# Inverse lengths of queries and keys: one GpSimd power over 16 columns a tile in place of two over 8

## The chip, the cores and the metric

The kernel runs on one core of a Trainium2 chip. The metric is the device time of one execution in microseconds. Several runs of a kernel are compared by their median.

## The reference

Sixteen sequences of 256 tokens with 128 features pass through six layers: a local-attention feed-forward (its output halved and added), a full attention with relative positions, the first again, a mixture of 64 experts, a state-space layer, and the experts again. The change lies in the first of them. There each token's projection is split into 8 heads of 64, queries and keys are divided by their length, and then rotated:

```python
def l2norm(t):
    return t / jnp.clip(jnp.linalg.norm(t, axis=-1, keepdims=True), 1e-12)
q = l2norm(q) * qs
k = l2norm(k) * ksc
q, k = rotary_xpos(q, k)
o = local_attention(q, k, v)
```

The layer has a depth of 2, and it is run twice.

## The kernel before

Two sequences (512 tokens, four tiles of 128) form a group; there are eight. Stages follow each other: `first_and_third` (local attention beside the experts of another group), `second` (full attention beside the state-space layer), `first_and_third` again. The groups are staggered, so most stages run two streams side by side. The order of the work is written out by hand for each engine.

`LocalFfn.run` (L1738) orders a stage. It has four passes (two layers of depth, two sequences each), each with two tiles of 128 tokens. A pass is projected (`project_*`), attended (`attend_*`) and mixed (`mix_*`), and the three phases of different passes overlap in rounds of eight steps r. Between them `beside` issues steps of the experts. A stage of the kind "first" in the middle of the run is entered with a `carry`: its pass 0 was projected in the stage before. All other stages are entered without one. Their pass 0 is projected at the entry, all steps in a row: VectorE runs `project_vector` for its four steps and then `beside.vector(dve, 2)` (L1861 to L1863); GpSimd runs `project_gpsimd` for both tiles (L1832); TensorE runs its five steps with filler matmuls between them (`keep_busy`, L137; L1750 to L1756). In the rounds, VectorE's steps come at r = 1 to 4 and GpSimd's tiles at r = 1 and 3.

The steps of one tile are these. TensorE projects queries, keys and values (L1380). ScalarE copies them (L1406, L1401) and squares queries and keys (L1409). VectorE sums the squares of each head to 16 lengths (L1433), clips them (L1435), and rotates: for the queries L1419, L1420, L1421, with the second step the same three lines for the keys, then adds the keys' two parts (L1441) and multiplies the keys by their inverse lengths (L1445). All these VectorE operations from L1419 on read two tensors of SBUF. GpSimd raises the clipped sums of squares to the power -0.5 in two instructions of 8 columns, keys first (L1452), adds the queries' parts (L1454) and multiplies the queries by their inverse lengths (L1458). TensorE transposes keys, then queries (L1387), in each of its steps 3 and 4, and ScalarE copies the result (L1412).

The semaphore `inv_norm` rises with each power. VectorE's key product waits for the first of a tile's two, GpSimd's query product for the second:

```python
dve.wait_ge(self.inv_norm, 2 * tile + 1)      # L1443
pool.wait_ge(self.inv_norm, 2 * tile + 2)     # L1456
```

After the tiles, attention reads the transposed keys and queries: scores (L1480) on a mask (L1476), their maxima on VectorE (L1577), exponentials on ScalarE (L1555), transposes and products on TensorE (L1509, L1520). Routing of the experts is a chain on VectorE (L625 to L644) with one exponential on ScalarE (L579); then each pair of experts has matmuls (L562, L568), a tanh (L586), a gate on VectorE (L654) and a product with the routing weights on GpSimd (L594). The state-space stages use GpSimd for sums of 1024 columns (L829, L844).

Of the kernel before, what the change touches and what calls it, by code (L numbers as in the profile page):

```python
# [10 lines left out]
ALU = mybir.AluOpType  # L11
# [12 lines left out]
DEPTH, LH, LD, WINDOW = 2, 8, 64, 64  # L24
# [1292 lines left out]
class LocalFfn:  # L1317
# [105 lines left out]
    def project_vector(self, dve, i, step):  # L1423
        v = self.nc.vector
        l, t = i // GROUP_SEQS, step // 2
        i -= self.first
        tile, lens = 2 * i + t, self.lens[t]
        if step % 2 == 0:
            dve.wait_ge(self.squared, tile + 1)
            if i >= 1:  # L1430
                dve.wait_ge(self.q_rotated, tile - 1)
                dve.wait_ge(self.projected, 10 * (i - 1) + 8 + 2 * t)
            v.tensor_reduce(lens, self.sine[t].rearrange("p (h d) -> p h d", d=LD), AX, ALU.add).then_inc(self.summed, 1)  # L1433
            dve.wait_ge(self.summed, tile + 1)
            v.tensor_scalar(lens, lens, 1e-24, None, ALU.max).then_inc(self.clipped, 1)  # L1435
            self.rotary(l, t, 0).then_inc(self.split, 1)
        else:
            self.rotary(l, t, 1).then_inc(self.k_split, 1)
            dve.wait_ge(self.k_split, tile + 1)
            keys = self.cosine[t][:, INNER:2 * INNER]  # L1440
            v.tensor_tensor(keys, keys, self.sine[t][:, INNER:2 * INNER], ALU.add).then_inc(self.k_added, 1)  # L1441
            dve.wait_ge(self.k_added, tile + 1)
            dve.wait_ge(self.inv_norm, 2 * tile + 1)  # L1443
            keys = keys.rearrange("p (h d) -> p h d", d=LD)
            v.tensor_tensor(keys, keys, lens[:, LH:].unsqueeze(2).broadcast_to([128, LH, LD]), ALU.mult).then_inc(self.k_rotated, 1)  # L1445

    def project_gpsimd(self, pool, i, t):
        b, tile = self.b, 2 * (i - self.first) + t
        lens, queries, sine = self.lens[t], self.cosine[t][:, 0:INNER], self.sine[t]
        pool.wait_ge(self.clipped, tile + 1)  # L1450
        for half in (lens[:, LH:], lens[:, 0:LH]):
            pool.tensor_tensor(half, half, b.minus_half[:].broadcast_to([128, LH]), ALU.pow).then_inc(self.inv_norm, 1)  # L1452
        pool.wait_ge(self.split, tile + 1)
        pool.tensor_tensor(queries, queries, sine[:, 0:INNER], ALU.add).then_inc(self.added, 1)  # L1454
        pool.wait_ge(self.added, tile + 1)
        pool.wait_ge(self.inv_norm, 2 * tile + 2)  # L1456
        queries = queries.rearrange("p (h d) -> p h d", d=LD)
        pool.tensor_tensor(queries, queries, lens[:, 0:LH].unsqueeze(2).broadcast_to([128, LH, LD]), ALU.mult).then_inc(self.q_rotated, 1)  # L1458

# [545 lines left out]
```

## Time and profile before

| | |
|---|---|
| median of three runs | 4873.61 us (4861.64 to 4876.70) |
| profiled execution | 4871.84 us, its span 4869.5 us |
| mean granted TensorE clock | 0.928 |
| tiles (one for each pass, two tiles each, 16 stages) | 128, with 256 powers |

The profile comes from one execution. A page has the busy time of each engine over the span, the costliest groups of instructions, and for each the idle time of the engine just before them, with the operation that ended it. PE is TensorE, DVE is VectorE, ACT is ScalarE, POOL is GpSimd. In a timeline, the first number is the start in us from the span's start, the second the duration; `x2` is two instructions in a row shown as one; a bracket gives the idle time before and what released the engine. An instruction's start is when the engine takes it up after its waits; one that is held back by another engine while running shows a longer duration.

### The profile page before, as it was taken

How to read it: one execution, taken by the hardware profiler on the slowest of the kernel's cores; microseconds unless marked ns; L12 is line 12 of the kernel's file. 1: busy time of each engine (PE TensorE's matmuls, PEld its weight loads, DVE VectorE, ACT ScalarE, POOL GpSimd, SP SyncE). 2: the span in 40 equal slices, each digit the busy share in tenths (PEclk: the TensorE clock that was granted, in tenths of full speed). 3: DMA queues.
4: the chain of work that ended last, by engine and by line, in shares of the span. 5: the costliest groups of instructions: out<-in, count | busy, mean ns of one | idle time of the engine just before them, and what ended most of it. 6: DMA issues, size and time to landing. Idle time of an engine off the chain costs nothing. (4 is left out here: it accounts for less than half of the span.)

```text
span 4869.5 us, 54706 instructions
## 1 busy us (share of the span) xinstructions
PE 4023.7 (83%) x17172; PEld 2422.5 (50%) x17172; DVE 3013.0 (62%) x5743; ACT 2787.0 (57%) x6184; POOL 2063.3 (42%) x1342
## 2 busy tenths in 40 slices
PE   6788898788878888888987988878887888889846
PEld 4446554455445554455544555445544555445412
DVE  4326666666576674766657666666747667476464
ACT  4465657555576555665665655755557555666332
POOL 2103244444264451644436434444436444165334
PEclk9898999999999999999999999999999999999867
DMA  3020013111131111210121111301113111221212
GB/s 102 1 89 1 22 50 122 30 44 40 34 122 41 35 46 63 86 49 29 58 85 61 53 30 49 122 29 44 38 36 122 41 35 49 68 76 49 81 47 75
DMA packets 188824, 274.01 MB, mean 56 GB/s; under 512 B 23448, under 2 KB 102900, under 8 KB 188532
## 3 DMA queue, kind: packets, MB, share of 16 engines
q1 hardware_dynamic: 186340, 268.72, 17.2%
q8 instruction: 147, 2.41, 0.2%
q10 hardware_dynamic: 2192, 1.70, 0.1%
q14 instruction: 145, 1.19, 0.1%
HBM read 215.54 MB, written 54.79 MB: 56 GB/s over the span
## 5 line engine op out<-in xcount | busy, mean ns | idle before, releaser
L594 POOL TENSOR_TENSOR work<-work 128x512 f32<-128x512 f32 x512 | 668.5, 1307 | 1200.8 <-DVE work L654 1117.5
L1452 POOL TENSOR_TENSOR work<-work,minus_half 128x8 f32<-128x8 f32 x256 | 469.5, 1848 | 545.2 <-DVE work L1435 542.9
L654 DVE SCALAR_TENSOR_TENSOR work<-work,psum 128x512 f32<-128x512 f32 x528 | 362.1, 686 | 412.9 <-ACT work L586 411.8
L562 PE MATMUL psum<-work,w_up 128*128 128x512 f32 x1024 | 546.2, 616 | 79.5 <-DVE work L654 76.0
L1555 ACT ACTIVATE work<-psum,work 128x128 f32<-128x128 f32 (+1 forms) x1024 | 392.3, 397 | 367.8 <-DVE work L1577 367.4
L586 ACT ACTIVATE work<-psum 128x512 f32<-128x512 f32 x528 | 315.3, 598 | 453.7 <-PE psum L562 433.4
L568 PE MATMUL psum<-work,w_down 128*128 128x512 f32 x1024 | 536.3, 606 | 5.5 <-POOL work L594 5.5
L1520 PEld LDWEIGHTS psum<-work 128*128 128x128 f32 x3072 | 388.6, 197 | 55.9 <-issue 54.1
L1520 PE MATMUL psum<-work 128*128 128x64 f32 x3072 | 410.3, 278 | 0.9 <-DVE work L1587 0.3
L1380 PE MATMUL psum<-wqkv,xn 128*128 128x512 f32 x768 | 374.8, 613 | 30.2 <-DVE xn L1685 26.3
L906 DVE TENSOR_TENSOR_SCAN work<-work,psum 128x256 f32<-128x256 f32 x512 | 323.1, 673 | 72.8 <-issue 35.1
L1509 PE MATMUL psum<-ident,work 128*128 128x128 f32 x1536 | 246.6, 285 | 140.0 <-ACT work L1555 110.6
L1509 PEld LDWEIGHTS psum<-ident,work 128*128 128x128 f32 x1536 | 185.1, 145 | 325.5 <-ACT work L1555 218.2
L844 POOL TENSOR_TENSOR pair<-pair,work 128x1024 f32<-128x1024 f32 x128 | 301.5, 2355 | 94.2 <-DVE work L829 85.4
L568 PEld LDWEIGHTS psum<-work,w_down 128*128 128x128 f32 x1024 | 195.7, 193 | 256.2 <-issue 218.3
L1641 PE MATMUL psum<-sq,w 128*128 128x256 f32 (+1 forms) x768 | 219.9, 429 | 73.1 <-DVE sq L1706 54.4
L1577 DVE TENSOR_REDUCE work<-psum 128x2 f32<-128x384 f32 (+1 forms) x384 | 212.4, 594 | 96.7 <-PE psum L1480 96.7
L562 PEld LDWEIGHTS psum<-work,w_up 128*128 128x128 f32 x1024 | 182.7, 194 | 173.0 <-DVE work L654 103.3
L829 POOL TENSOR_TENSOR work<-work,rows 128x1024 f32<-128x1024 f32 x28 | 66.1, 2361 | 417.4 <-DVE work L906 417.4
L1012 PE MATMUL psum<-rel_k,work 128*128 128x384 f32 x512 | 199.3, 517 | 45.5 <-ACT work L1099 27.2
L1433 DVE TENSOR_REDUCE work<-work 128x16 f32<-128x1024 f32 x128 | 155.4, 1214 | 126.4 <-ACT work L1409 125.5
L1406 ACT COPY work<-psum 128x512 f32<-128x512 f32 x256 | 148.6, 597 | 145.3 <-PE psum L1380 145.3
(228 smaller groups left out, 8503.7 us busy)
## 6 DMA issues: line engine op xcount, KB each, us to landing
work<-expert_weight_rows SPq DMA_DIRECT2D x1024, 128.0 KB, 2.9
position_scores<-work SPq DMA_DIRECT2D x64, 768.0 KB, 3.5
work<-position_scores SPq DMA_DIRECT2D x64, 512.0 KB, 3.8
work<-state_readout_rows SPq DMA_DIRECT2D x72, 256.0 KB, 4.3
rows<-state_readout_rows SPq DMA_DIRECT2D x32, 256.0 KB, 3.9
sq<-state_readout_rows SPq DMA_DIRECT2D x24, 256.0 KB, 4.2
rows<-in_L_attn_q SPq DMA_DIRECT2D x8, 256.0 KB, 2.9
expert_weight_rows<-work SPq DMA_DIRECT2D x16, 128.0 KB, 2.3
```

Source lines behind the costliest of these rows:

```text
L562: nc.tensor.matmul(UP, b.w_up[:, p * 128:(p + 1) * 128], self.xn, start=True, stop=True).then_inc(self.up, 1)
L568: nc.tensor.matmul(SUM, b.w_down[:, q], self.gate_h[q % 3], start=q == 0, stop=False).then_inc(self.down, 1)
L586: nc.scalar.activation(self.tanh_h[p % self.turns][0:rows], bank(b, self.ups[p % self.turns])[0:rows], ACT.Tanh, scale=0.5).then_inc(self. ...
L594: pool.tensor_tensor(h, h, self.weights[p % self.SLOTS], ALU.mult).then_inc(self.gated, 1)
L654: v.scalar_tensor_tensor(out=self.gate_h[p % 3][0:rows], in0=self.tanh_h[p % self.turns][0:rows], scalar=1.0, in1=bank(b, self.ups[p % sel ...
L844: pool.tensor_tensor(self.sums, self.sums, self.state_pairs[n % 2], ALU.add).then_inc(self.added, 1)
L906: ins = v.tensor_tensor_scan(self.states[i % 4][:, at], self.decays[i % 2][:, at], drive[:, at], 0.0, ALU.mult, ALU.add)
L1380: nc.tensor.matmul(out, b.xn[:, at:at + 128], b.wqkv[:, l, part * INNER:(part + 1) * INNER], start=True, stop=True).then_inc(self.projecte ...
L1452: pool.tensor_tensor(half, half, b.minus_half[:].broadcast_to([128, LH]), ALU.pow).then_inc(self.inv_norm, 1)
L1509: ins = nc.tensor.transpose(bank(b, 2)[:, n * 128:(n + 1) * 128], flat[:, n * 128:(n + 1) * 128], b.ident[:])
L1520: ins = nc.tensor.matmul(bank(b, 3)[:, head * LD:(head + 1) * LD], self.probs_t[m % 2][:, n * 128:(n + 1) * 128], self.v_sb[i % 2][:, c, h ...
L1555: ins = self.nc.scalar.activation(out[:, x, -n:] if t else out[:, x], self.scores(m)[:, x], ACT.Exp, bias=self.neg_max[i % 2][:, slot:slot ...
```

## The change

The two powers of 8 columns become one of 16, over the whole tile `lens` (queries' lengths in columns 0 to 7, keys' in 8 to 15). Both waits on `inv_norm` become waits for this one instruction; the number of increments per tile falls from two to one. Nothing else is touched.

```diff
@@ project_vector
-            dve.wait_ge(self.inv_norm, 2 * tile + 1)
+            dve.wait_ge(self.inv_norm, tile + 1)
@@ project_gpsimd
-        for half in (lens[:, LH:], lens[:, 0:LH]):
-            pool.tensor_tensor(half, half, b.minus_half[:].broadcast_to([128, LH]), ALU.pow).then_inc(self.inv_norm, 1)
+        pool.tensor_tensor(lens, lens, b.minus_half[:].broadcast_to([128, 2 * LH]), ALU.pow).then_inc(self.inv_norm, 1)
@@
-        pool.wait_ge(self.inv_norm, 2 * tile + 2)
+        pool.wait_ge(self.inv_norm, tile + 1)
```

## Rows read from the trace of the kernel before

**Rows 1.** The page, part 1: busy time (share of the span), instructions of each engine

```profile
PE 4023.7 (83%) x17172; PEld 2422.5 (50%) x17172; DVE 3013.0 (62%) x5743; ACT 2787.0 (57%) x6184; POOL 2063.3 (42%) x1342
```

**Rows 2.** The page, part 5: the costliest groups; busy us, mean ns | idle before

```profile
L594 POOL TENSOR_TENSOR work<-work 128x512 f32<-128x512 f32 x512 | 668.5, 1307 | 1200.8 <-DVE work L654 1117.5
L1452 POOL TENSOR_TENSOR work<-work,minus_half 128x8 f32<-128x8 f32 x256 | 469.5, 1848 | 545.2 <-DVE work L1435 542.9
...
L844 POOL TENSOR_TENSOR pair<-pair,work 128x1024 f32<-128x1024 f32 x128 | 301.5, 2355 | 94.2 <-DVE work L829 85.4
```

**Rows 3.** The waits of TensorE: us in total, times, longest

```profile
PE psum L1387 <- POOL work L1458: 18.2, 17, 1.6
```

**Rows 4.** Timeline of VectorE, 894 to 916 us and near 4374: start us, us, what

```profile
896.02 0.17 DVE L1435 TENSOR_SCALAR work<-work 128x16 f32<-128x16 f32 x1
...
899.51 0.69 DVE L1445 TENSOR_TENSOR work<-work 128x512 f32<-128x512 f32 x1
...
901.45 1.55 DVE L1419 TENSOR_TENSOR work<-work,rope_w 128x512 f32<-128x512 f32 x1
902.93 0.42 DVE L1420 TENSOR_TENSOR work<-work,rope_w 128x256 f32<-128x256 f32 x1
...
905.72 0.69 DVE L1445 TENSOR_TENSOR work<-work 128x512 f32<-128x512 f32 x1
906.32 0.42 DVE L625 TENSOR_TENSOR work<-psum,expert_bias 128x256 f32<-128x256 f32 x1
...
908.32 0.61 DVE L633 TENSOR_TENSOR work<-work 128x256 f32<-128x256 f32 x1
...
912.76 1.28 DVE L1577 TENSOR_REDUCE work<-psum 128x4 f32<-128x512 f32 x2
...
4374.28 0.42 DVE L625 TENSOR_TENSOR work<-psum,expert_bias 128x256 f32<-128x256 f32 x1
```

**Rows 5.** Timeline of GpSimd, 896.2 to 909 us

```profile
896.28 3.62 POOL L1452 TENSOR_TENSOR work<-work,minus_half 128x8 f32<-128x8 f32 x2 [5.55 <-DVE work L1435]
899.87 1.47 POOL L1454 TENSOR_TENSOR work<-work 128x512 f32<-128x512 f32 x1
901.41 1.04 POOL L1458 TENSOR_TENSOR work<-work 128x512 f32<-128x512 f32 x1
902.41 3.70 POOL L1452 TENSOR_TENSOR work<-work,minus_half 128x8 f32<-128x8 f32 x2
906.08 1.45 POOL L1454 TENSOR_TENSOR work<-work 128x512 f32<-128x512 f32 x1
```

**Rows 6.** Timelines of ScalarE and TensorE, 910 to 914 us

```profile
913.54 0.37 ACT L1555 ACTIVATE work<-psum,work 128x128 f32<-128x128 f32 x1 [3.49 <-DVE work L1577]
...
910.64 1.16 PE L1480 MATMUL psum<-work 64*128 64x128 f32 x16
```

**Rows 7.** The instructions of three lines: ns min/median/max, first and last start us

```profile
L1452 POOL TENSOR_TENSOR work<-work,minus_half x256: 1628/2017/2129, 43.1 to 4495.8; 128x8 f32<-128x8 f32 x128
...
L1454 POOL TENSOR_TENSOR work<-work x128: 1256/1472/2131, 46.7 to 4497.4; 128x512 f32<-128x512 f32 x128
...
L1419 DVE TENSOR_TENSOR work<-work,rope_w x256: 674/684/1553, 42.9 to 4496.4; 128x512 f32<-128x512 f32 x128
```

**Rows 8.** TensorE by microseconds: length, busy (instructions), granted clock, DMA; and its timeline there

```profile
1099.00:1100.00 1.00, 0.00 (x0) 0.80 0.00 0
...
1100.79 2.50 PE L1641 MATMUL psum<-sq,w 128*128 128x256 f32 x5 [3.31 <-DVE sq L1706]
```

**Rows 9.** Timelines of GpSimd and VectorE, 1098 to 1106 us

```profile
1098.77 4.06 POOL L1452 TENSOR_TENSOR work<-work,minus_half 128x8 f32<-128x8 f32 x2 [2.69 <-DVE work L1435]
1102.80 1.79 POOL L1454 TENSOR_TENSOR work<-work 128x512 f32<-128x512 f32 x1
...
1102.77 0.69 DVE L1445 TENSOR_TENSOR work<-work 128x512 f32<-128x512 f32 x1
...
1105.12 0.48 DVE L1711 SCALAR_TENSOR_TENSOR work<-psum,vec_cols,work 128x256 f32<-128x256 f32 x1 [1.22 <-ACT work L1675]
```

## The prediction

> **What bounds the kernel now.** I read the totals first. TensorE works 83% of the span and GpSimd 42% [rows 1], so no engine is full: the end is set by chains of waits that run through all of them. The edited powers are GpSimd's second largest group, 256 instructions and 469.5 us [rows 2]. If every saved microsecond reached the end the change would be large, so the question is who waits for GpSimd's rotation. The table of TensorE's waits answers it: 17 waits, 18.2 us in all [rows 3]. All but these few of the 128 tiles are ready before TensorE asks. 18.2 us is 0.37% of the time, the ceiling of what earlier queries can give directly.
>
> The 17 waits lie in nine places: the entries of stages without a carry, where both tiles of pass 0 are projected with nothing between them. They start at 43.1 us [rows 7], at 359 and, in the groups after, from 896 to 4364. Seven of the nine have expert routing right behind the second tile on VectorE, the first at 906.32 and the last at 4374.28 [rows 4]; the other two, the one at 43.1 among them, have none. I take the entry at 896 as the pattern. GpSimd: power pair 896.28 to 899.90, addition L1454, multiplication L1458, then tile 1 the same way [rows 5]. VectorE runs without idle time from the clip at 896.02 to the score maxima at 912.76, and ScalarE's exponentials then wait 3.49 us for these maxima [rows 4, 6]. So behind the entry **VectorE's chain sets the pace**, not GpSimd's.
>
> The rows also show how the two engines disturb each other. L1419 on VectorE (two SBUF inputs) starts at 901.45, 0.04 after GpSimd's L1458, and takes 1.55 us where its median is 0.68; L1458 ends at 902.45, and L1419 ends 0.55 later [rows 4, 5, 7]. In the other order, L1445 starts at 899.51, 0.36 before L1454, and keeps its 0.69; L1454 then takes 1.47 instead of 1.26 [rows 4, 5, 7]. Whoever starts first keeps the other out to the end. During the power itself the rotations of VectorE are not stretched. The Trainium skill (SBUF — State Buffer, "Who interferes with whom") says the same as a rule: an exclusive lock between GpSimd and a VectorE instruction with two SBUF inputs, and issue order decides who blocks. By that rule, as by the rows, the order in which L1445 and L1454 start matters more here than the power's length.
>
> **The change, part by part.**
>
> *The power.* Two instructions of 8 columns take 2.02 and 1.63 us and together 3.62 [rows 5, 7]. The merged one costs the first plus eight more columns. No row shows 16 columns. From above: if nothing of the second instruction is fixed cost, 3.6 us. From below: if all of it is fixed, 2.0. The nearest fixed part is that of GpSimd's ordinary tensor_tensor: 1.307 us for 512 columns and 2.355 for 1024 leave 0.26 [rows 2], so the other 1.37 of the 1.63 is columns. I take 2.02 + 1.37 = **3.4 us**, 0.2 less than the pair, as these are the same engine and kind of instruction.
> The Trainium skill (GPSIMD Engine Reference, "Elementwise — side-by-side cycle accounting") gives about 2.6 cycles an element at 1.2 GHz, by which eight columns would cost 17 ns and the merged power 2.0 us; the sum by that is the second rival below.
>
> *The keys' wait.* Before, VectorE's key product L1445 needed only the first half, ready at 898.3; it started at 899.51 with no wait. Now it needs the whole power: 896.28 + 3.4 = 899.68, plus 0.08 for the signal (the lag from the clip's end at 896.19 to the power) = 899.76. That is only 0.25 later. But GpSimd's L1454 stands directly behind the power and needs no signal from VectorE; it follows its predecessor's end by minus 0.03 [rows 5]. It starts at 899.65, **ahead of** L1445, where it used to start 0.36 behind. It runs 1.27 us, to 900.92, and L1445 ends at 901.47 instead of 900.20: 1.27 late.
>
> *Tile 1.* Behind L1445 on VectorE stand the second reduction, the clip and the rotation. L1419 moves from 901.45 to 902.72. GpSimd's L1458 is over by then (about 902.4), so L1419 loses its stretch of 0.87 and the next operation, L1420, comes at 903.32 against 902.93: 0.39 late. The power of tile 1 now waits for the clip: 902.89 to 906.29. L1445 could start at 906.11, is released at 906.37 and finds L1454 (906.26 to 907.53) ahead again: it ends at 908.08 against 906.41, 1.67 late. Queued behind it are the routing (L625 on) and the maxima. L633 (0.61) has shown a stretch of 0.19 that goes, as L1458 is over. Net 1.48 us per entry, on the chain that ScalarE and through it TensorE wait for: 7 x 1.48 = **+10.4 us**.
>
> *The two other entries.* Nothing follows the product on VectorE. GpSimd's L1458 of tile 1 ends about 0.34 late (held by the locked L1445), and TensorE waits for that: +0.4 together.
>
> *TensorE's clock.* In an entry TensorE will now stand idle some 3 us between its filler and the key transposes, 1.5 more than before. A gap of 3.31 us comes with a fall of the granted clock (0.80 in one microsecond of it, on its way from 2.4 to 1.2 GHz) [rows 8]. The score matmuls (1.16 us for 16) [rows 6] would take up to twice as long, but VectorE's maxima are late anyway. Bounds: 0, and 7 x 1.2 = 8 us; I take 2, nearer to the covered case.
>
> *The other 110 tiles.* There L1445 starts 4.0 us or more after the power's start (shortest: 1102.77 behind 1098.77) [rows 9], so no new wait. The adds start 0.2 earlier, and operations locked behind them are free 0.2 earlier; most adds are themselves held by an L1419 that started first, so they don't move. Bounds -3 and 0, I take -1. In the tiles like the one at 1098 us L1445 (1102.77) starts only 0.03 before L1454; there the order flips too and costs VectorE about 0.9, but it idles 1.22 us before its next dependent step [rows 9], which covers it. Without that cover nine such tiles would cost 8 us.
>
> *Removed instruction and semaphore steps* cost and give nothing beyond the above; no DMA or queue of SyncE is touched.
>
> **Sum.** 10.4 + 0.4 + 2 - 1 = +11.8 us. The profiled execution took 4871.84 us (span 4869.5 and 2.3 around it), 1.8 below the median of the runs. 4871.8 + 11.8 + 1.8 = **4885.4 us**, 0.24% slower than 4873.61. A measurement of this kernel tells about 0.3%, 14.6 us, from no change, so this is the upper part of "no change".
>
> **The rivals.**
> 1. *The saving arrives* (faster). If L1445 keeps its turn, or its lateness reaches nobody, only GpSimd's shorter chain counts. With the power at 3.4 it gives 16 x 0.2 = 3 us, 4870, which is no change. To be faster the power must be near 2.0 us: then the 17 waits vanish, 18.2 us, and the time is **4855**. It decides at a saving of about 0.9 us a tile. Against it: L1454 starts ahead of L1445 for every length below 3.6.
> 2. *Columns nearly free and more collisions* (clearly slower). With a power of 2.0 both adds start inside VectorE's key steps, L1441 and L1445: two stretches of 0.87 a tile, 3.5 an entry, less 0.87 for L1419 and 0.2 for L633: 2.4 x 7 = 17 us, with the clock's 2 **4892**. For it: the same lock rows; against: it needs the low bound of the power.
> 3. *Late but covered.* The lock is as told but ScalarE or TensorE absorb the 1.5 us within the pass, or the power takes as long as before and the order stays mixed: **4873**. For it: 83% busy TensorE; against: TensorE idles behind exactly these exponentials.
> 4. *The change doesn't do what it says*: the merged instruction falls into a costlier form, over 4 us. Each 0.5 us above 3.6 costs two tiles in nine entries, 9 us. Little speaks for it.
>
> **How the numbers follow.** Forecast 0.62, rival 1 at its fast end 0.05, rival 2 0.13, rival 3 0.18, rival 4 0.02. The forecast's own spread is 4876 to 4895 (clock term, share absorbed), about two fifths of it beyond 4888.2. Slower: 0.62 x 0.4 + 0.13 x 0.8 + 0.02 = 0.37; faster 0.05; the rest, 0.58, within 0.3%. The range 4867 to 4899 leaves out the fast end and the worst of rival 2.
>
> **What would show it.** In the profile after: 128 powers of 128x16 at 3.4 us (2.0: rival 2 or 1; over 4: rival 4). At the nine entries L1445 of both tiles at 1.4 to 1.7 us instead of 0.69, starting about 0.1 after L1454; L1419 of tile 1 back at 0.68; the routing 1.5 to 1.7 us later behind the clip; the maxima still without idle time before them. TensorE's waits for L1458 stay near 18 us. The forecast is wrong if L1445 keeps 0.69, or if the pass behind the entry ends no later than before.

## The result and the profile after

| | kernel before | changed kernel |
|---|---|---|
| median, us (6 runs each) | 4876.23 (4861.64 to 4880.01) | 4915.15 (4906.55 to 4916.76) |
| ratio after / before | | 1.008, 95% interval [1.0066, 1.0094] |
| profiled execution, us | 4871.84 (span 4869.5) | 4915.54 (span 4913.0) |
| TensorE busy, us | 4023.7 | 4054.9 |

The change costs 39 us. The forecast was 4885.4 with a range up to 4899, so the sign was right, the "no change" that was put first (0.58) was not, and the time lies outside the range.

Part 1 of the page after, and the groups of its part 5 that answer to [rows 1, 2]; from the power on, line numbers are one lower than before:

```profile
PE 4054.9 (83%) x17172; PEld 2446.0 (50%) x17172; DVE 3061.3 (62%) x5743; ACT 2788.9 (57%) x6184; POOL 2012.7 (41%) x1214
...
L594 POOL TENSOR_TENSOR work<-work 128x512 f32<-128x512 f32 x512 | 667.0, 1303 | 1245.4 <-DVE work L654 1181.4
L1451 POOL TENSOR_TENSOR work<-work,minus_half 128x16 f32<-128x16 f32 x128 | 419.6, 3278 | 574.0 <-DVE work L1435 571.7
```

The joined power takes 3.28 us, and GpSimd is busy for 50.6 us less. All of that and more turns up elsewhere: VectorE is busy for 48 us more with the same 5743 instructions, and TensorE for 31 us more with the same 17172 matmuls. Nothing was added for either. So VectorE's instructions were stretched, and TensorE's ran longer: of the 43.5 us of span, 31.2 are matmuls that took more time and 12.3 are idle.

The waits of TensorE's transposes (total us, times, longest) show where its waits for the rotation went. Two rows of the kernel before, beside the one of [rows 3], and the three after:

```profile
PE psum L1387 <- ACT work L1412: 10.1, 7, 1.4
PE psum L1387 <- DVE work L1445: 6.5, 9, 1.4
```

```profile
PE psum L1387 <- ACT work L1412: 21.4, 7, 3.1
PE psum L1387 <- DVE work L1445: 17.9, 11, 2.5
PE psum L1387 <- POOL work L1457: 2.7, 10, 0.3
```

The waits for GpSimd's query product, 18.2 us before [rows 3], shrank to 2.7, but the three together grew from 34.8 to 42.0 us: the transposes now wait for the keys instead. At the entry shown below, the first tile's queries are ready some 0.2 us earlier behind the first clip and the second tile's no earlier at all, so little was there to gain.

**An entry.** The timelines of VectorE, GpSimd and TensorE at the entry that was the pattern of [rows 4, 5]:

```profile
900.54 0.17 DVE L1435 TENSOR_SCALAR work<-work 128x16 f32<-128x16 f32 x1
...
904.18 1.67 DVE L1445 TENSOR_TENSOR work<-work 128x512 f32<-128x512 f32 x1 [0.19 <-POOL work L1451]
...
910.65 1.67 DVE L1445 TENSOR_TENSOR work<-work 128x512 f32<-128x512 f32 x1 [0.19 <-POOL work L1451]
912.24 0.41 DVE L625 TENSOR_TENSOR work<-psum,expert_bias 128x256 f32<-128x256 f32 x1
...
919.33 1.29 DVE L1576 TENSOR_REDUCE work<-psum 128x4 f32<-128x512 f32 x2 [0.76 <-PE psum L1479]
```

```profile
900.79 3.28 POOL L1451 TENSOR_TENSOR work<-work,minus_half 128x16 f32<-128x16 f32 x1 [5.55 <-DVE work L1435]
904.04 1.26 POOL L1453 TENSOR_TENSOR work<-work 128x512 f32<-128x512 f32 x1
```

```profile
913.61 1.97 PE L1387 MATMUL psum<-ident,work 128*128 128x128 f32 x8 [3.06 <-ACT work L1412]
916.25 1.03 PE L1475 MATMUL psum<-mask_bf,ident_bf 128*128 128x512 bf16 x2 [0.68 <-ACT work L1412]
917.22 2.08 PE L1479 MATMUL psum<-work 64*128 64x128 f32 x16
```

GpSimd's addition starts at 904.04, VectorE's key product 0.14 later, and the product ends at 905.85, 0.55 after the addition. From the clip of tile 0 to the routing (L625) it is 11.70 us, against 10.30 before. TensorE then runs its 16 score matmuls in 2.08 us instead of 1.16 [rows 6], and the maxima (L1576) wait 0.76 for them. Before, they waited at none of the seven entries with routing; now they wait at two.

**A stage's end.** The same two engines and TensorE in the second of two tiles projected ahead, 10 us before the next stage:

```profile
1692.91 1.77 DVE L1441 TENSOR_TENSOR work<-work 128x512 f32<-128x512 f32 x1
1694.71 1.41 DVE L1445 TENSOR_TENSOR work<-work 128x512 f32<-128x512 f32 x1
1696.05 0.86 DVE L1710 SCALAR_TENSOR_TENSOR work<-psum,vec_cols,work 128x256 f32<-128x256 f32 x2
```

```profile
1689.62 3.28 POOL L1451 TENSOR_TENSOR work<-work,minus_half 128x16 f32<-128x16 f32 x1 [3.15 <-DVE work L1435]
1692.87 1.26 POOL L1453 TENSOR_TENSOR work<-work 128x512 f32<-128x512 f32 x1
```

```profile
1704.71 1.06 PE L1475 MATMUL psum<-mask_bf,ident_bf 128*128 128x512 bf16 x2
```

The addition is 0.04 us ahead of VectorE's key *addition* (L1441), which takes 1.77 instead of 0.69, and the query product then stretches the key product to 1.41: 1.8 us more, where before neither was touched [rows 9]. The idle time before the second L1711 (1.22 us in [rows 9], 1.01 at this place) is gone, and the next stage's mask matmuls take 1.06 where the kernel before took 0.59.

Counted from this clip to the next stage's first, the next stage begins 2.4 to 2.8 us later at five of the seven such places, 1.9 later at one, and 0.2 earlier at the one of [rows 9]. This lateness goes with the clock and not with the stretch. The stretches from clip to clip, first in the kernel before at this place and at that of [rows 9], then here after the change, then the same place in entries_only, a run told below that leaves these tiles as they were (length, busy time of PE, PEld, DVE, ACT and POOL, granted clock, DMA):

```profile
1681.21:1702.44 21.23, 16.08 (x72) 10.04 (x72) 12.06 (x25) 11.14 (x30) 8.53 (x8) 0.92 0.05 14
1098.51:1122.78 24.27, 18.77 (x72) 12.08 (x72) 12.06 (x25) 11.27 (x30) 8.53 (x8) 0.79 0.04 12
```

```profile
1689.37:1713.44 24.07, 19.05 (x72) 12.15 (x72) 13.74 (x24) 11.14 (x30) 7.55 (x7) 0.79 0.04 12
```

```profile
1689.23:1713.21 23.98, 18.82 (x72) 12.19 (x72) 11.96 (x24) 11.28 (x30) 8.44 (x8) 0.79 0.04 12
```

Leaving out the first place, which has fewer matmuls, two of six took about 24 us before, all six 24 or more after, and five of six about 24 in entries_only, whose key addition and product kept 0.69 there. After the change the clock was already at 0.50 from 1691 to 1692 us, before the stretched addition starts at 1692.91. What the 1.8 us cost the next stage by themselves is therefore not shown.

### The profile page after: what moved, and what is told of

Its sections match the earlier page's. It is cut to its first block and busy times, and to the rows that moved or that the text cites. A ratio compares the mean times of both kernels' runs of the same rounds, so it can differ in the third digit from the quotient of the medians.

```text
span 4913.0 us, 54578 instructions
## 1 busy us (share of the span) xinstructions
PE 4054.9 (83%) x17172; PEld 2446.0 (50%) x17172; DVE 3061.3 (62%) x5743; ACT 2788.9 (57%) x6184; POOL 2012.7 (41%) x1214
## 5 line engine op out<-in xcount | busy, mean ns | idle before, releaser
L1451 POOL TENSOR_TENSOR work<-work,minus_half 128x16 f32<-128x16 f32 x128 | 419.6, 3278 | 574.0 <-DVE work L1435 571.7
L1576 DVE TENSOR_REDUCE work<-psum 128x2 f32<-128x384 f32 (+1 forms) x384 | 212.5, 595 | 104.9 <-PE psum L1479 104.9
```

What stands on the lines that cost most here:

```text
L1451: pool.tensor_tensor(lens, lens, b.minus_half[:].broadcast_to([128, 2 * LH]), ALU.pow).then_inc(self.inv_norm, 1)
```

## The experiments

Kernels of one batch ran on the same chip beside the kernel before. Medians of the kernel before were 4878.9, 4865.6, 4872.5 and 4868.7 us in the four batches, so each kernel is read by its ratio. Theory A throughout: the loss is VectorE's, from an order of instructions that turned at particular tiles.

### First batch: where is the loss, and is it the order?

**late_keys**: two powers as before; only the wait of the key product changes.

```diff
-            dve.wait_ge(self.inv_norm, 2 * tile + 1)
+            dve.wait_ge(self.inv_norm, 2 * tile + 2)
```

> Two powers of 8 columns as before; only the keys' product (L1445) waits for the second of them too. GpSimd's addition L1454 starts when it did before. Theory A (start order: whoever starts first shuts the other out): at the nine entries L1445 is released at the power pair's end plus 0.08, now behind L1454, and takes about 1.7 us instead of 0.69; routing of tile 1 is 1.5 to 2 us later there; all other tiles keep their order, as L1445 comes 4.0 us or more behind the power. Total +12 to +16 us, 1.0025 to 1.0035. Theory B (the loss of the change comes from GpSimd's additions starting 0.34 us earlier all over the rounds): +0 to +3 us. Theory C (it is the wait itself, 0.2 to 0.4 us in eighteen tiles): +4 to +7 us.

Measured: 4899.09 us, ratio 1.0048 [1.0034, 1.0062], some 20 us, more than expected. No GpSimd time was saved, yet half of the loss is there. One thing was not foreseen: the stage's end turned as well, VectorE first and GpSimd below:

```profile
1686.02 0.69 DVE L1441 TENSOR_TENSOR work<-work 128x512 f32<-128x512 f32 x1
1686.90 1.68 DVE L1445 TENSOR_TENSOR work<-work 128x512 f32<-128x512 f32 x1 [0.19 <-POOL work L1452]
```

```profile
1682.74 4.06 POOL L1452 TENSOR_TENSOR work<-work,minus_half 128x8 f32<-128x8 f32 x2 [2.69 <-DVE work L1435]
1686.77 1.26 POOL L1454 TENSOR_TENSOR work<-work 128x512 f32<-128x512 f32 x1
```

The second power ends 4.06 us behind the start, just after the 4.0 at which the key product used to start, and that is enough to let the addition go first. Whether this accounts for the surplus over the 12 to 16 us is not shown: the next run's product is as long there, and that run lost 7 us in all.

**padded**: the joined power with a GpSimd memset behind it, all else as in the change.

```diff
         pool.tensor_tensor(lens, lens, ... ALU.pow).then_inc(self.inv_norm, 1)
+        pool.memset(b.spare[:, 0:192], 0.0)
```

> The change as it is, one power of 16 columns, with a memset of 192 columns of a scratch tensor behind it on GpSimd, about 0.34 us (128 columns took 0.25), which reads no memory. GpSimd's addition starts again about 3.6 us behind the power's start, as in the kernel before, and the keys are released at 3.36, ahead of it. Theory A: every order is again that of the kernel before; ratio 0.998 to 1.002. Theory B (additions starting earlier) says the same. Theory C (a longer wait for the keys, or a cost of the merged instruction itself): the loss stays, 1.006 to 1.009.

Measured: 4886.06 us, ratio 1.0014 [1.0005, 1.0024]. Work of 0.22 us *added* to GpSimd took back some 30 of the 39 us. At the entry the key product is ahead again, by 0.06 us, and takes 0.69:

```profile
902.68 0.69 DVE L1446 TENSOR_TENSOR work<-work 128x512 f32<-128x512 f32 x1 [0.18 <-POOL work L1452]
```

```profile
902.52 0.25 POOL L1454 MEMSET spare<- 128x192 f32 x1
902.74 1.76 POOL L1456 TENSOR_TENSOR work<-work 128x512 f32<-128x512 f32 x1
```

The wider power itself is therefore not what costs most of the time. What is left, 7 us, is clear of noise, and so it is with the two longer pads below. At the seven entries the stretch to the next pass is still 2 us longer in all, by this run's profile.

**entries_only** and **not_entries**: the joined power only in the 18 tiles of the nine entries (pass 0, projected at its own stage's entry), or in the other 110. `is_ahead` is set for a pass 0 that is projected in the stage before.

```diff
-        for half in (lens[:, LH:], lens[:, 0:LH]):
+        whole = i == 0 and not self.is_ahead     # not_entries: the opposite
+        for part in ((lens,) if whole else (lens[:, LH:], lens[:, 0:LH])):
     ...     # the power over part; inv_norm rises by 2 where it is whole, by 1 otherwise
```

> The merged power in the nine entries of stages only (pass 0 projected at the entry, 18 tiles), two powers in the other 110 tiles. Theory A with the places as I count them: between the clip of tile 0 and the next pass each routing entry is 1.2 to 2.1 us later, so +10 to +16 us, 1.002 to 1.0035, about a third of the whole loss of 39 us. Theory that the entries are the whole loss: +35 to +40 us. Theory that they are covered: 0.

> The complement: two powers in the nine entries, the merged power in the other 110 tiles. Theory A: the order of GpSimd's addition and VectorE's rotation flips there too, because 0.34 us are saved and not 0.2: L1441 at 1.77 and L1445 at 1.42 us in the last tile before a stage ends, L1421 at 1.49 in the second tile of rounds. +22 to +30 us, 1.0045 to 1.006. My forecast's step (the other tiles do not lose) says -3 to 0 us.

Measured: 1.0029 [1.0016, 1.0041] and 1.0058 [1.0044, 1.0071], by medians +15 and +26 us, together 41. The loss has two homes, and the larger one is not at the entries. Where it lies can be read from VectorE's key operations (L1419 to L1421 for the keys, L1441, L1445), summed over tiles in the profiles of the kernel before and the change: 52.1 and 69.6 us in the 18 tiles of the entries (less 7.5 us that the queries' rotation gained there), 53.0 and 66.5 in the 14 projected ahead, 474.5 and 500.3 in the 96 of the rounds.

### Second batch: inside the larger part

**ahead_only** (`whole = self.is_ahead`) and **rounds_only** (`whole = i > 0`), 14 tiles in seven stages (the expectation counts 12 in six) and 96 tiles:

> The joined power only in the 12 tiles projected ahead of their pass (two in each of six stages), two powers elsewhere. Theory A (order and lock at particular tiles): in the last tile before a stage's end the query addition now starts 3.2 instead of 4.1 us behind the clip, ahead of VectorE's key addition, and both key operations are stretched (0.69 to about 1.8 and 1.4); the stage's end has 1.2 us of cover for 1.8, and in five of the six the next stage's first matmuls run at the lower clock, 2.4 to 2.8 us a stage in the changed kernel's profile: +8 to +16 us on the kernel before. Rival D (the stage ends only inherit lateness of what runs before them, the loss is spread over the rounds): within 4 us of the kernel before.

> The joined power only in the tiles projected inside the rounds of attention (every tile but a layer's first two and those projected ahead), two powers elsewhere. Theory A: VectorE is stretched in about half of these tiles but they lie in stages where something else ends last, so the rest of the 26 us that the kernel without the entries lost: +6 to +16 us. Rival D: nearly all of the 26 us, +20 or more. Rival E (only entries and stage ends count): within 4 us.

Measured: 4891.66 us, 1.0051 [1.0037, 1.0066], and 4887.01 us, 1.0046 [1.0033, 1.0059]. Each alone loses more than expected, together 47 us where the run that held both lost 26. The parts don't add up; one reading is that a stretch which runs at the lower clock for one reason doesn't lose it again for the other, but no run tells that. Rival E falls. Rival D falls by ahead_only, which it had within 4 us, but rounds_only meets its sign of 20 us or more: the rounds do lose, and they are not all of the loss.

**padded_long**: as padded, with eight memsets of 64 columns, 0.75 us.

> The joined power with eight GpSimd memsets of 64 columns behind it, in all tiles: 0.8 to 1.0 us more ahead of the query addition, so that it starts 4.1 to 4.3 us behind the start of the power, at or behind where the second of two powers used to let it go at its latest. Theory A: VectorE's key addition and product are first in the last tile of a stage again (0.69 both), where the shorter pad still left a product of 1.64; the entries stay as before: 0 to +6 us on the kernel before, unless queries that come 0.5 us later in the tiles of the rounds hold something up. Rival C (the wider power itself costs time): +25 us or more.

Measured: 4875.07 us, 1.002 [1.0007, 1.0034], 9.5 us on the kernel before by medians, above the 6 expected. But the key product was still long, since the addition came 0.06 us *before* it (2845.72 against 2845.78):

```profile
2845.78 1.74 DVE L1446 TENSOR_TENSOR work<-work 128x512 f32<-128x512 f32 x1
```

```profile
2841.77 3.28 POOL L1452 TENSOR_TENSOR work<-work,minus_half 128x16 f32<-128x16 f32 x1 [2.69 <-DVE work L1436]
2845.00 0.75 POOL L1454 MEMSET spare<- 128x64 f32 x8
2845.72 1.26 POOL L1456 TENSOR_TENSOR work<-work 128x512 f32<-128x512 f32 x1
```

**queries_behind_keys**: the joined power, and an explicit order in the 32 tiles of a stage's pass 0, at an entry or ahead.

```diff
         pool.wait_ge(self.split, tile + 1)
+        if i == 0:
+            pool.wait_ge(self.k_rotated, tile + 1)
```

> The joined power everywhere; in a pass's own first two tiles and in those projected ahead GpSimd's query addition waits until VectorE's key product of the same tile is done. Theory A: no key operation is stretched there any more, and GpSimd, undisturbed, does the two query operations in 1.04 us each, so queries are ready no later than in the kernel before; what is left is the loss of the rounds: +4 to +14 us on the kernel before, 25 to 35 us below the change. If the loss sits in the rounds (rival D), it stays within 10 us of the change's time.

Measured: 4903.5 us, 1.0077 [1.0062, 1.0091]: a miss. The key products took 0.69 in these tiles, as meant. But in tile 1 of an entry the joined power starts only when the queries of tile 0 are done, and now waits in series: the key product waits 0.52 us for it, and the queries wait for the product. The seven entries are 7.9 us late in all for it, so the order alone is no cure where the power itself is late. That is a fifth of the 38 us. The run lies within 10 us of the change's time, which the expectation had named as rival D's sign, and the 96 tiles of the rounds, where no wait was set, keep the change's key operations (498.6 us).

### Third batch: the order as a lever

**two_powers_ahead_behind** and **two_powers_rounds_behind**: the kernel *before*, with the order written down.

```diff
         pool.wait_ge(self.split, tile + 1)
+        if self.is_ahead and t == 0:             # rounds: i > 0 or self.is_ahead and t == 0
+            pool.wait_ge(self.k_rotated, tile + 1)
```

> The kernel before with one wait added: in the first of the two tiles projected ahead of a pass (six stages) GpSimd's query addition waits until VectorE's key product is done. Theory A (a fixed order decides what VectorE pays): the two operations that VectorE runs beside that addition in the kernel before (1.49 and 1.42 us instead of 0.41 and 0.69) shrink by 1.8 us a stage, and that is on the chain to the stage's end: 4 to 14 us faster than the kernel before. Rival F (such a wait only moves the time to GpSimd's queries): within 4 us of it. Rival G (a later query product delays the second tile's powers and the stage's end): 4 us slower or more.

> The same wait in the tiles projected inside the rounds of attention too (not in a pass's own first two, not in the second one ahead). Theory A: VectorE loses its stretched key operations there, 0.7 to 1.8 us in about half of 104 tiles, of which the change's own run says that perhaps half counts: another 5 to 30 us faster than the run with the wait ahead only. Rival H (in the rounds GpSimd is held up behind VectorE's later work, and queries come last): slower than that run by 5 us or more.

Measured: the first 4871.19 us, 0.9997 [0.9984, 1.0011], no gain. In the 14 tiles ahead VectorE's key operations took 12.5 us less, 1.8 a stage, as meant. But GpSimd's query product now ran beside the second tile's rotation of the queries and held one step of it, 1.26 us instead of 0.42:

```profile
1104.08 1.26 DVE L1422 TENSOR_TENSOR work<-work,rope_w 128x256 f32<-128x256 f32 x1
```

That took 5.9 of the 12.5 us back, and why the other 6.6 did not reach the end stays open. The second **4802.67 us, 0.9856 [0.9834, 0.9879]**, 70 us faster than the kernel before, over twice the most that was expected, and the fastest form found. Its part 1 shows VectorE 157 us less busy with the same instructions:

```profile
PE 4009.0 (83%) x17172; PEld 2403.0 (50%) x17172; DVE 2856.0 (59%) x5743; ACT 2784.9 (58%) x6184; POOL 2005.0 (42%) x1342
```

One tile of a round, VectorE's side of the keys, first in the kernel before, then here:

```profile
650.17 1.49 DVE L1420 TENSOR_TENSOR work<-work,rope_w 128x256 f32<-128x256 f32 x1
651.59 1.26 DVE L1421 TENSOR_TENSOR work<-work,rope_w 128x256 f32<-128x256 f32 x1
652.88 1.65 DVE L1441 TENSOR_TENSOR work<-work 128x512 f32<-128x512 f32 x1
654.56 0.69 DVE L1445 TENSOR_TENSOR work<-work 128x512 f32<-128x512 f32 x1
```

```profile
638.96 0.42 DVE L1422 TENSOR_TENSOR work<-work,rope_w 128x256 f32<-128x256 f32 x1
639.29 0.42 DVE L1423 TENSOR_TENSOR work<-work,rope_w 128x256 f32<-128x256 f32 x1
639.75 0.69 DVE L1443 TENSOR_TENSOR work<-work 128x512 f32<-128x512 f32 x1
640.47 0.69 DVE L1447 TENSOR_TENSOR work<-work 128x512 f32<-128x512 f32 x1
```

5.1 us became 2.2, because neither of GpSimd's two operations came beside them; its addition started at 641.31, behind them all. Over the 96 tiles of the rounds the key operations fell from 474.5 to 278.4 us.

**queries_behind_keys_all**: the same as queries_behind_keys, in every tile.

> The joined power with that wait in every tile. If the loss of the rounds is VectorE's stretch, as theory A has it, this is 10 to 25 us below the same form with the wait in a pass's first tiles and those ahead alone, which lost 38 us to the kernel before; if it is something else (the clock alone, queries that come late), within 5 us of that.

Measured: 4839.7 us, 0.9938 [0.9917, 0.9959]: 64 us below the form with the wait in the first tiles alone, well beyond the 10 to 25 expected, and the joined power with this wait is faster than the kernel before.

**padded_twelve**: twelve memsets of 44 columns, 0.90 us.

> The joined power with twelve memsets of 44 columns behind it, 0.85 to 0.95 us instead of 0.75: the query addition starts 4.05 to 4.2 us behind the start of the power, where the key product of the last tile before a stage's end starts at 4.01. Theory A: with the addition behind it, that product takes 0.69 us again, where eight memsets (addition at 3.95) left it 1.74: a flip by 0.1 us of GpSimd's time. The time stays within 5 us of the run with eight memsets, since that product's 1.05 us had 1.25 us of cover. Rival I (the product is long for another reason): still over 1.4.

Measured: 4879.83 us, 1.0022 [1.0004, 1.004]. The flip is there. VectorE, then GpSimd:

```profile
2842.26 0.69 DVE L1442 TENSOR_TENSOR work<-work 128x512 f32<-128x512 f32 x1
2842.99 0.69 DVE L1446 TENSOR_TENSOR work<-work 128x512 f32<-128x512 f32 x1
```

```profile
2838.97 3.28 POOL L1452 TENSOR_TENSOR work<-work,minus_half 128x16 f32<-128x16 f32 x1 [2.69 <-DVE work L1436]
2842.21 0.90 POOL L1454 MEMSET spare<- 128x44 f32 x12
2843.06 1.74 POOL L1456 TENSOR_TENSOR work<-work 128x512 f32<-128x512 f32 x1
```

With these runs the last tile before a stage's end has a scale, by the time from the start of the power to the start of the query addition:

| form | addition behind the power's start, us | key addition, key product, us |
|---|---|---|
| joined (the change) | 3.25 | 1.77, 1.41 |
| one memset (padded) | 3.45 | 0.69, 1.64 |
| eight memsets | 3.95 | 0.69, 1.74 |
| two powers (before) | 4.03 | 0.69, 0.69 |
| twelve memsets | 4.09 | 0.69, 0.69 |

From clip to clip, and without the first place, the next stages of the one-memset form took about 24 us at two of six, as in the kernel before, and those of the eight-memset form 21.3 to 22.3 at all six, so a product 1 us longer was covered. With none, all six took 24 or more; that the 1.8 us did it is not shown, as said above. And all three padded forms are 7 to 10 us above the kernel before: with twelve memsets, which put the order of this tile right, the seven entries are 5.6 us late in all, by the profile.

### Fourth batch: the two forms with the order fixed

Two kernels take two_powers_rounds_behind and join the power, in every tile but the 18 of the entries (`whole = i > 0 or self.is_ahead`), or in all; a repeat of it is the measure.

> The same kernel as two_powers_rounds_behind, as the measure for the two beside it: 0.983 to 0.988 of the kernel before, 4795 to 4812 us.

> two_powers_rounds_behind with the joined power in every tile but a pass's own first two. In the tiles of the rounds and the first ahead GpSimd's addition can no longer come ahead of VectorE's key product, whatever the power takes; without that wait the same step cost 26 us. Theory A (the joined power loses there by the order alone): within 6 us of the kernel with two powers and the wait, apart from the six last tiles before a stage's end, which the wait does not cover: 0 to +12 us. Rival J (the keys' later inverse lengths, or the clock, cost it in the rounds too): +16 us or more.

> two_powers_rounds_behind with the joined power in every tile. Theory A: the entries are uncovered by the wait, so on top of joined_not_entries_behind come their 13 us as before, of 12.9 us that the two profiles showed at seven of them: 13 to 25 us above two_powers_rounds_behind, not the 39 us that the same step cost without the wait. Rival J: 35 us or more.

| | median, us | ratio to the kernel before | TensorE busy, us |
|---|---|---|---|
| two_powers_rounds_behind_2 | 4805.09 | 0.9872 [0.9854, 0.9891] | 3992.0 |
| joined_not_entries_behind | 4805.28 | 0.9869 [0.985, 0.9888] | 3996.6 |
| joined_rounds_behind | 4839.65 | 0.9934 [0.9918, 0.995] | 4037.5 |

In the rounds and ahead, the joined power that cost 26 us costs 0.2 once GpSimd cannot go ahead of the key product; the four times of each form lie between 4800 and 4809 us. In the last tile ahead, which has no such wait, the product still took 1.64, and it was covered. Rival J falls there: neither the keys' later lengths nor the power did it. But it saves nothing either. At the entries, which the wait does not cover, the same step costs 34 us, more than the 13 to 25 expected and just short of the 35 that the expectation gave rival J, so at the entries J is not refuted. From clip to clip each routing entry is 2.1 us late, 15 us over seven (12.9 in the change's own profile). TensorE's busy time is 41 us more than in joined_not_entries_behind, by the two profiles, so the loss stands in matmuls that take longer, some of them far from any entry. The first row is joined_not_entries_behind from the first clip of the tiles ahead to the next stage's first, the second the same part of the work in joined_rounds_behind, 7.0 us later at its start and 8.9 at its end:

```profile
1648.95:1678.97 30.02, 23.18 (x93) 13.15 (x91) 20.81 (x39) 16.89 (x39) 13.50 (x10) 0.94 0.03 10
```

```profile
1655.92:1687.82 31.90, 25.33 (x95) 14.95 (x93) 20.82 (x39) 17.42 (x39) 13.49 (x10) 0.89 0.03 9
```

The forms are the same there; only the stage's entry, some 180 us earlier, differs. Its 2.1 us of delay stayed as they were over the 114 us that followed. Here the granted clock is 0.89 instead of 0.94, a larger share of the stretch at 1.2 GHz, and TensorE is busy for 25.3 us instead of 23.2. That the entry's delay is what leads to it was not tested by itself, and each form has one profile.

## Why the prediction was right and wrong

- **The lock and the order at the entries: right.** Both key products came 0.13 to 0.14 us behind the addition, took 1.67 and ended 0.55 behind it; L1419 of tile 1 was back at 0.69, and the routing came 1.40 us later behind the clip (1.67 foreseen), which late_keys, padded and entries_only bear out from three sides.
- **The entries' sum: right in the profile, low in the runs.** Forecast 10.4 + 0.4 + 2 = 12.8 us. From the first clip to the first of the next pass the seven entries lost 1.2 to 2.1 us each, 12.9 in all. The score matmuls, the step that the clock term named, took 2.08 us at six of the seven (at one before); at five of these six the loss is 2.1. Alone (entries_only) they cost 15 us, with the order fixed elsewhere 34.
- **The power: a little long.** 3.4 foreseen, 3.28 measured. Against the pair at 3.62 that is 0.34 saved and not 0.2; against the pair of 4.06 [rows 9], whose second power took 2.07 and not 1.63, it is 0.78. The 0.12 mattered out of all proportion: by 3.4 the addition at a stage's end would have started behind L1441 and stretched L1445 alone, as padded and padded_long did; by 3.28 it started 0.04 ahead of L1441 and stretched both.
- **"The other 110 tiles: I take -1, bounds -3 and 0": this step failed.** They cost 26 us (not_entries). The prediction saw the flip at a stage's end and its price of 0.9 under a cover of 1.22; the price was 1.8. For the other tiles it took it that most additions are held by an L1419 that started first and so don't move, and that the rest only free VectorE earlier. Both were wrong: additions held up by VectorE (over 1.31 us instead of 1.26) fell from 89 of the 110 tiles to 60, and in 73 of the 110 the rotation step that starts next behind the addition is another one than before. The 96 tiles of the rounds had no row of their own. In tiles of the rounds the earlier addition met one operation more: in a second tile at 662 us L1441 and L1445 took 1.64 and 1.41 before, and L1421, L1441 and L1445 1.49, 1.42 and 1.64 after. joined_not_entries_behind shows that with the order fixed nothing is left of the 26.
- **The clock term was too small for the kernel as a whole.** It allowed up to 8 us, at entries. TensorE's busy time grew by 31 us. I gave the clock no share outside the entries, though [rows 8] had shown a fall beside a gap at a stage's end.
- **The rivals.** The fast rival needed a power of 2.0 us; the waits for L1458 did nearly vanish (18.2 to 2.7 us), against the sign that they stay near 18, and the kernel still got slower: they went over to the keys, so this ceiling said nothing of what earlier queries give. The second rival's mechanism, two stretched key operations in one tile, is what happened at the stages' ends, though not at the entries and not by a power of 2.0.
- **The cost of the power from the Trainium skill.** The Trainium skill (GPSIMD Engine Reference, "Elementwise — side-by-side cycle accounting") has about 2.6 cycles an element, measured on an addition, and the prediction's estimate from it was 2.0 us. The measured 3.28 is 1.26 above a single power of 8 columns, 0.16 us a column: the measurement decides against that figure for the power.
- **The lock.** The Trainium skill (SBUF — State Buffer, "Who interferes with whom") has the issue order decide who blocks. The scale above agrees: between additions at 3.95 and 4.09 us, a product that starts at 4.01 falls from 1.74 to 0.69. But not every GpSimd instruction that reads SBUF keeps VectorE out. Beside the power from 900.79 to 904.07 us, whose inputs lie in SBUF too, VectorE's rotation steps kept 0.41 to 0.69; no run tells why.

Still open: how the 26 and 15 us divide into stretched instructions and a lower clock that follows them (only their sum was measured), where the 6.6 us that the wait in the first tiles ahead spared VectorE went, what the 7 to 10 us of the padded forms are beyond their entries, and what the best wait for the entries would be; no form was tried that helps them.

## What to carry to other kernels

Where GpSimd and VectorE both read two operands from SBUF, a shorter instruction on one is a change of order first and a saving second: list every place where the two come within the saved time of each other, tile by tile, before pricing it. If the order matters, write it down with a semaphore; here one wait was worth 1.4%, and it made the disputed edit harmless where it applied. And look at busy time of engines whose instructions did not change: growth there (48 us on VectorE, 31 on TensorE) names the loss before any timeline is read.

## What the hardware showed that was not expected

- A GpSimd power costs 2.02 us for 8 columns when it starts on an idle engine, 1.63 right behind another [rows 5, 7] (but 2.07 in nine of 128), and 3.28 for 16, with a spread of only 9 ns over 128 instructions. Joining two saves 0.34 us, and 0.78 in those nine.
- 0.22 us a tile of added GpSimd work, doing nothing, took the ratio from 1.008 to 1.0014, some 30 us.
- Memsets beside a VectorE instruction with two SBUF inputs did not lengthen it: the key addition at 2842.26 took 0.69 with padded_twelve's memsets running from 2842.21 to 2843.11.
- The losses of two places did not add: 26 and 21 us apart, 26 together; and the entries' was 15 us in one surrounding and 34 in another, while their own delay was nearly the same. By the profiles, from two fifths of a form's loss to all of it stood in TensorE's busy time, with the same 17172 matmuls.
- The same work between two clips took 21.2 us at a granted clock of 0.92 and 24.0 at 0.79, and the kernel before had both.
